# New joint order of the four engines within a step of the transformer layers: both projections directly behind the outputs, the feed-forward sum one position forward

## The reference, cut to what matters

```python
def attn_layer(x, Wqkv, qs, ksc, Wo):       # 6 layers of these two
    q, k, v = split(x @ Wqkv, 3)            # 16 heads of 64
    q, k = l2norm(q) * qs, l2norm(k) * ksc
    q, k = rotary(q, scale), rotary(k, 1 / scale)
    return local_attention(q, k, v) @ Wo    # windows of 32, looking one window back

def ffn_layer(x, g, bln, W1, b1, W2, b2):
    a, gate = split((layernorm(x) * g + bln) @ W1 + b1, 2)
    return a * gelu(gate) @ W2 + b2

def reference(x, ...):
    x = layernorm(x + first_attention(x))   # causal, only the diagonal of the softmax weighs v
    y = x
    for i in range(6):
        y = attn_layer(shift_tokens(y), ...) + y
        y = ffn_layer(shift_tokens(y), ...) + y
    return layernorm(x + y)
```

## Time and profile before

| | |
|---|---|
| median of 3 runs | 3484.91 us (3483.71 to 3487.97) |
| profiled execution | 3485.04 us, span of its instructions 3483.2 us |
| TensorE matmul busy | 3410.3 us, 98% |
| ScalarE busy | 3056.1 us, 88% |
| VectorE busy | 2991.3 us, 86% |
| GpSimd busy | 2494.3 us, 72% |
| DMA | 160.59 MB, mean 46 GB/s |
| granted TensorE clock, mean | 0.997 |

### The profile page before, as it was taken

How to read it: one execution, slowest core, us unless ns; L and a number is a source line. 1 busy time by engine, 2 the same in 40 slices (tenths; PEclk the granted TensorE clock), 3 DMA queues, 4 the chain that set the end, 5 groups by cost and what they waited for, 6 DMA issues and landing times. The chain is left out here.

```text
span 3483.2 us, 177745 instructions
## 1 busy us (share of the span) xinstructions
PE 3410.3 (98%) x70388; PEld 2881.8 (83%) x70388; DVE 2991.3 (86%) x7016; ACT 3056.1 (88%) x10549; POOL 2494.3 (72%) x2057
## 2 busy tenths in 40 slices
PE   8999999999999999999999999999999999999998
PEld 5666677888888888888888888888888888888877
DVE  8999988888888888888888888888888888888886
ACT  8999978898988888888888888888888889888886
POOL 0121178887878878788787887878888788887874
PEclk9999999999999999999999999999999999999999
DMA  2000011111211111121111121111211111111111
GB/s 105 8 5 20 5 53 53 48 42 43 57 55 50 44 44 46 54 57 48 46 44 50 52 57 47 43 42 54 59 48 46 43 47 54 45 46 47 51 42 44
DMA packets 177474, 160.59 MB, mean 46 GB/s; under 512 B 113933, under 2 KB 124813, under 8 KB 176397
## 3 DMA queue, kind: packets, MB, share of 16 engines
q1 hardware_dynamic: 176653, 149.22, 15.2%
HBM read 25.71 MB, written 4.19 MB: 9 GB/s over the span
## 5 line engine op out<-in xcount | busy, mean ns | idle before, releaser
L1544 POOL TENSOR_TENSOR a_rn<-a_ssqc,a_minus_half 128x16 f32<-128x16 f32 x384 | 1113.4, 2900 | 256.3 <-DVE a_ssqc L1751 252.1
L1428 ACT ACTIVATE late<-bank,a_negmax 128x64 f32<-128x64 f32 x3072 | 963.9, 343 | 31.0 <-DVE a_negmax L1705 29.4
L1562 POOL TENSOR_TENSOR a_r<-a_u,a_rn 128x512 f32<-128x512 f32 x768 | 800.7, 1043 | 55.9 <-DVE a_u L1733 10.5
L1428 ACT ACTIVATION_READ_ACCUMULATOR late<-bank,a_negmax 128x1 f32 x3072 | 728.6, 237 | 0.0
L1717 DVE TENSOR_TENSOR a_u<-bank,a_rot_c 128x512 f32<-128x512 f32 x768 | 524.7, 683 | 175.3 <-ACT a_sq L1404 174.7
L1551 POOL TENSOR_TENSOR a_PN<-late,a_erec 128x256 f32<-128x256 f32 x768 | 487.9, 636 | 255.8 <-DVE a_erec L1758 241.4
L1726 DVE TENSOR_TENSOR a_v<-bank,a_rot_s 128x512 f32<-128x512 f32 x768 | 522.7, 681 | 0.0
L1733 DVE TENSOR_TENSOR a_u<-a_u,a_v 128x1024 f32<-128x1024 f32 x384 | 469.7, 1223 | 25.6
L1404 ACT ACTIVATE a_sq<-bank 128x512 f32<-128x512 f32 x768 | 462.8, 647 | 17.2 <-PE bank L1013 16.7
L1411 ACT ACTIVATE a_QK<-bank 128x512 f32<-128x512 f32 x768 | 465.8, 607 | 4.1 <-PE bank L1054 1.9
L1054 PE MATMUL bank<-ident,a_r 128*128 128x128 f32 x3072 | 463.3, 274 | 5.2 <-ACT late L1396 1.8
(11 more groups left out here) (190 smaller groups left out, 7757.2 us busy)
## 6 DMA issues: line engine op xcount, KB each, us to landing
a_V_sh<-a_V_nat SPq DMA_DIRECT2D x384, 192.0 KB, 2.5
a_V_sh<-a_V_nat SPq DMA_DIRECT2D x192, 64.0 KB, 2.4
late<-in_qkv SPq DMA_DIRECT2D x20, 384.0 KB, 3.7
a_x_sh<-X SPq DMA_DIRECT2D x48, 128.0 KB
a_V_sh<-a_V_nat SPq DMA_DIRECT2D x192, 32.0 KB, 2.1
a_x_sh<-X SPq DMA_DIRECT2D x48, 127.0 KB
late<-X SPq DMA_DIRECT2D x47, 128.0 KB
late<-X SPq DMA_DIRECT2D x47, 127.0 KB
```

Of the source, the lines that this page charges most:

```text
L1428: ins = act.activation(E[:, s.par, k, :], scores[:, hp, col:col + KW], ACT.Exp, bias=negmax[:, s.par, k:k + 1], accum_out=esum[:, s.par, k ...
L1544: pool.tensor_tensor(rn[:, a.par, :], ssqc[:, a.par, :], minus_half[:, :], ALU.pow).then_inc(S["rn"], 1)
L1562: pool.tensor_tensor(heads(r[:, a.par, half]), heads(u[:, a.par, half]), rn[:, a.par, mm * 2 * HG:(mm + 1) * 2 * HG].unsqueeze(2).to_broad ...
```

## The change

The order within a step changes on all four engines. No instruction that computes is added or removed.

- TensorE: `project` of tile 1 follows `project` of tile 0 in every step (in steps 3 and 7 a piece of `up` stood between them). The other pieces come next, most of them ahead of `values`: in step 6 both `up`, in step 7 `transpose_x` and then `up`, in step 4 one ahead of `values` and the other too.
- ScalarE: `exps` (0,1) moves behind (1,1), so the copies of queries and keys (tile 0) and of the outputs come one group of exps earlier. `gelu` goes ahead of the squares, `gate_out` 1 behind both squares, `high_x` between them, the splits of weights ahead of `values` and `probs`.
- VectorE: `sines` before `cosines` for both tiles, with other work between them for tile 0; `clamp` behind both; `reciprocals` of head pair 1 earlier, of 0 at the end; `stats` behind `add`; `product` moved; `feed_forward_out` from the head of step 6 into the middle of step 5 (behind `add` and a reciprocal, ahead of `sines`, `cosines` and the other reciprocal).
- GpSimd: `units` of tile 1 first, `deviation` one step later.
- Waits: since the cosines now come last, `project` waits for them too (u_rot); the logits and the maxima wait for exp0 beside exp1; `sines` waits for the squares as `cosines` does.

The diff, without its hunk headers' context beyond the functions:

```diff
--- before.py
+++ after.py
@@ -1007,6 +1007,7 @@
                         pe.wait_ge(S["w_lo"], G * a.layer + a.g + 1)
                     ge(pe, S[f"sq{mm}"], a.k)
                     ge(pe, S[f"v_rot{mm}"], a.k)
+                    ge(pe, S["u_rot"], 2 * a.k - 1 + mm)
                     x, m = n % 2, slice((2 * a.half + mm) * P, (2 * a.half + mm + 1) * P)
                     pe.matmul(p_qk[mm][:, :], xh[:, x, m], wh[:, a.g, 0:2 * CQ], start=True, stop=False)
                     pe.matmul(p_qk[mm][:, :], xl[:, x, m], wh[:, a.g, 0:2 * CQ], start=False, stop=False)
@@ -1149,30 +1150,31 @@
                 late_end(n, p)
                 outputs(pair_at(n, p, LAG_O), n * NP + p, done(n, p - 1, LAG_T1))
                 project(n, p, 0)
+                project(n, p, 1)
+                if p == P_VALUES:
+                    up(n, p, 0, 1, p_ta)
+                if p == P_VALUES:
+                    up(n, p, 1, 1, p_tb)
+                if p == P_X and n + 1 < NI:
+                    transpose_x(n + 1)
+                if p == P_TURN:
+                    turn(n)
+                if p == P_GATES:
+                    up(n, p, 1, 0, p_ta)
+                if p == P_X:
+                    up(n, p, 2, 1, p_ta)
                 if p == P_GATE:
                     up(n, p, 0, 0, p_ta)
-                if p == P_X:
-                    up(n, p, 2, 1, p_ta)
-                project(n, p, 1)
-                if p == P_TURN:
-                    turn(n)
-                if p == P_VALUES:
-                    up(n, p, 0, 1, p_ta)
                 if p == P_GATES:
-                    up(n, p, 1, 0, p_ta)
+                    up(n, p, 2, 0, p_tb)
                 values(n, p)
                 late_pieces(n, p)
                 if p == P_BIAS:
                     shifts(n)
-                if p == P_X and n + 1 < NI:
-                    transpose_x(n + 1)
-                if p == P_VALUES:
-                    up(n, p, 1, 1, p_tb)
-                if p == P_GATES:
-                    up(n, p, 2, 0, p_tb)
                 if p == P_GELU:
                     down(n)
                 if s:
+                    ge(pe, S["exp0"], s.k)
                     ge(pe, S["exp1"], s.k)
                 logits(s, p_s)
                 transpose_probs(n, p)
@@ -1201,6 +1203,7 @@
                 if j == -3:
                     for name in ("sq0", "sq1", "v_rot0", "v_rot1"):
                         pe.wait_ge(S[name], NI * NP)
+                    pe.wait_ge(S["u_rot"], 2 * NI * NP)
                 else:
                     pe.wait_ge(S["exp1"], s.k if j == -4 else s.k - 1)
                 logits(s, end_s(s))
@@ -1443,32 +1446,32 @@
                     late_outputs(2 * p - 1)
                 queries_and_keys(pair_at(n, p, LAG_Q1), 1)
                 exps(s, 0, 0, p_s)
-                exps(s, 0, 1, p_s)
                 queries_and_keys(pair_at(n, p, LAG_Q0), 0)
                 exps(s, 1, 0, p_s)
                 outputs(pair_at(n, p, LAG_O))
                 exps(s, 1, 1, p_s)
+                if p < 2:
+                    split_up(n, p)
+                exps(s, 0, 1, p_s)
+                if p == P_GELU:
+                    gelu(n)
                 if p == P_TURN:
                     turned(n)
                 squares(n, p, 0)
+                if p == P_GATE:
+                    gate_out(n, 0, p_ta)
+                if p == P_X and n + 1 < NI:
+                    high_x(n + 1)
+                squares(n, p, 1)
                 if p == P_GATES:
                     gate_out(n, 1, p_ta)
-                if p == P_GELU:
-                    gelu(n)
-                if p == P_GATE:
-                    gate_out(n, 0, p_ta)
-                squares(n, p, 1)
                 if p == P_GATES:
                     gate_out(n, 2, p_tb)
-                if p == P_X and n + 1 < NI:
-                    high_x(n + 1)
-                values(n, p)
-                probs(pair_at(n, p, LAG_PT))
-                if p < 2:
-                    split_up(n, p)
                 split = split_at(n, p)
                 if split:
                     split_qkv(*split)
+                values(n, p)
+                probs(pair_at(n, p, LAG_PT))
 
             def end_exps(j, hp):
                 s = end_pair(j)
@@ -1564,13 +1567,13 @@
                                        ALU.mult).then_inc(S[f"r{mm}"], 1)
 
             def cycle(n, p):
+                units(pair_at(n, p, LAG_R + 1), 1)
                 probs(pair_at(n, p, LAG_S + 1), 0)
-                units(pair_at(n, p, LAG_R + 1), 1)
+                if p == P_NORM + 1 and n >= 2:
+                    deviation(n - 2)
                 probs(pair_at(n, p, LAG_S + 1), 1)
                 power(pair_at(n, p, LAG_R))
                 units(pair_at(n, p, LAG_R), 0)
-                if p == P_NORM and n >= 2:
-                    deviation(n - 2)
                 if p == 2 and n >= NI - 4:
                     last_deviation(n - NI + 4)
                 if (n, p) == (1, 0):
@@ -1701,6 +1704,7 @@
             def maxima(s, scores):
                 if s:
                     dve.wait_ge(S["logits"], s.k + 1)
+                    ge(dve, S["exp0"], s.k - 1)
                     ge(dve, S["exp1"], s.k - 1)
                     dve.tensor_reduce(negmax[:, s.par, :].rearrange("p (b i) -> p b i", b=2), scores.rearrange("p b (i k) -> p b i k", i=4), AX.X,
                                       ALU.max, negate=True).then_inc(S["max"], 1)
@@ -1720,7 +1724,10 @@
             def sines(a, mm):
                 if a:
                     m = 2 * a.half + mm
+                    dve.wait_ge(S[f"sq{mm}"], a.k + 1)
                     ge(dve, S["u"], a.k)
+                    if a.first and a.g == 0:
+                        ge(dve, S["rot"], MT * (a.layer - 1) + m + 1)
                     halves = lambda t: t.rearrange("p (s h t f) -> p s h t f", s=2, h=HG, t=2)
                     tab = rot_s[:, m, :, :].rearrange("p s (t f) -> p s t f", t=2).unsqueeze(2).to_broadcast([P, 2, HG, 2, DH // 2])
                     dve.tensor_tensor(halves(v[:, mm * 512:(mm + 1) * 512]), halves(p_qk[mm][:, :])[:, :, :, ::-1, :], tab,
@@ -1780,40 +1787,40 @@
 
             def cycle(n, p):
                 s, a, b = pair_at(n, p, LAG_S), pair_at(n, p, 0), pair_at(n, p, LAG_R)
-                if p == P_GELU + 1:
-                    feed_forward_out(n)
                 maxima(s, p_s)
                 norms(b)
+                sines(b, 1)
                 cosines(b, 1)
                 clamp(b)
-                sines(b, 1)
                 if p == P_X:
                     residual(n)
+                if p == P_TURN:
+                    norm(n)
+                add(b)
                 if p == P_NORM:
                     stats(n)
                 if p == P_TURN:
-                    norm(n)
-                add(b)
-                if p == P_X:
-                    product(n, 2, p_ta)
+                    turned(n)
+                reciprocals(s, 1)
                 if p == P_VALUES:
                     product(n, 0, p_ta)
-                if p == P_TURN:
-                    turned(n)
-                cosines(a, 0)
+                if p == P_VALUES:
+                    product(n, 1, p_tb)
+                if p == P_GELU:
+                    feed_forward_out(n)
                 sines(a, 0)
                 if p == P_BIAS:
                     biases(n)
+                if p == P_X:
+                    product(n, 2, p_ta)
                 if p == P_X and n + 1 < NI:
                     low_x(n + 1)
-                if p == P_VALUES:
-                    product(n, 1, p_tb)
+                if p == P_GATES:
+                    split_up(n)
+                cosines(a, 0)
                 reciprocals(s, 0)
-                reciprocals(s, 1)
                 if p in (P_TURN, P_GATES, P_GELU):
                     split_qkv(n, p)
-                if p == P_GATES:
-                    split_up(n)
                 if p == 3 and n >= NI - 4:
                     last_norm(n - NI + 4)
                 if p == 2 and n >= NI - 4:
```

## The result

| | before | after |
|---|---|---|
| median of 5 runs | 3484.59 us (3483.71 to 3487.97) | 3544.09 us (3542.22 to 3545.47) |
| profiled execution: span | 3483.2 us | 3542.3 us |
| TensorE busy | 3410.3 us | 3422.5 us |
| GpSimd busy | 2494.3 us | 2761.0 us |

The ratio is 1.0168 [1.0154, 1.0183]: 59.5 us slower, where the forecast was 24 us faster, and outside the range given. TensorE's mean granted clock is 0.996 for 0.997; by the granted clock of the two traces the lower level cost at most 14.1 us in after and 9.0 us in before, so it accounts for 5 us at most.

The account below looks back on a forecast made before the run. TensorE's instruction order was taken to set the pace, so only its gaps could be won. Terms -30 - 9 - 5 + 12 + 7.5 + 1 = -23.5, say -24 us, gave 3461 us; range 3444 to 3486.

Parts of the forecast that it names:

- the sentence on GpSimd: GpSimd: clamp 0.6 us later, transposes keep over half a microsecond of margin; priced nil, bounds 0 to 0.1 us a step.
- Deviation and normalisation: GpSimd's deviation moves one step on; normalisation in step 2 still finds it about 0.1 us ahead; priced nil.
- Step 2, priced at nothing: Step 2 of each iteration: no loss forecast, apart from +0.6 us once per layer for the qkv weights' low parts.
- step 6: TensorE's late starts around feed-forward and values matmuls vanish: 0.65 us in 46 iterations, -30 us, bounds 0 and -30.
- step 7: Next x transposed earlier, so TensorE's wait for VectorE's low part goes: 0.19 us in 46 iterations, -9 us.
- the edges: Second projection in steps 3 and 6 barely meets VectorE's cosines: +0.13 us each, 46 times, +12 us; bounds 0 to 0.4 each.
- the low weights: Low parts of qkv weights on VectorE, steps 2 and 5, five layers: 1.5 us each, +7.5 us, bounds 3 and 10.
- the high weights: Weights' high parts on ScalarE, moved ahead of values and probs, stop delaying a copy: -5 us, bounds 0 and -6.
- The first: Rival: VectorE 0.3 us later at steps 3 and 6, stalls 0.4 to 0.45 us, +40 instead of +12; chance 0.13.
- The second: Rival: added waits cost 0.11 to 0.18 us in each of 384 steps, 3503 to 3530 us; chance 0.15 with its like.
- a chain through ScalarE: Loss through ScalarE's order, priced at nil in the forecast; included in the second rival's chance of 0.15.
- The fourth: Rival: longer waits bring TensorE's clock another half-rate stretch, at most +7 us, 3468 us; chance 0.08.

Follow-up runs that it names:

- b_split: `b_clamp` with VectorE's `add` of 1024 columns cut into two of 512; 3497.94 us, ratio 1.0038.
- a_clamp: The kernel after, with only the clamp moved back between the two rotations of tile 1; 3473.26 us, ratio 0.9963.
- b_clamp: The kernel before, with only the clamp moved behind both rotations of tile 1; 3522.34 us, ratio 1.0104.
- a_pool: The kernel after, with only GpSimd's order as before (probs of head pair 0 first, deviation at the end of step 1); 3523.72 us, ratio 1.0116.
- b_gain: The kernel before, with only the moves for steps 6 and 7 and the waits for exp0; 3444.88 us, ratio 0.9885.
- b_waits: The kernel before, with only added TensorE waits: a third on each projection, a second ahead of the logits; 3482.31 us, ratio 0.9997.

## Why the prediction was wrong, point by point

- **The step that failed** is the sentence on GpSimd: "the clamp comes 0.6 us later ... the transposes wait for none of it by more than half a microsecond of margin ... Nil". The clamp's delay of 0.6 us was right, and of itself cost nothing in steps 0 and 3 (`b_split`). What was missed is beside what the instruction then runs: it starts with the `add` and is held for 0.96 us. This was outside the bounds given (0 to 0.1 us a step). `a_clamp` prices it at 71 us in the new order, `b_clamp` at 36 us in the old one.
- **Why it reaches TensorE.** GpSimd's work per step is 2 x 0.57 (probs) + 2 x 1.02 (units) + 3.03 (power) = 6.2 us. With 0.96 more (`power` in step 0) or 1.05 more (`probs` in step 1) it is 7.2, against 6.6 to 6.8 us of TensorE in these steps. It fits into steps 4 to 7, which last 7.7 to 9.3 us, and only just into step 3 (7.35), which still lost 0.43 us. A mean hid this: 72% over the whole span, and even the 81% of the middle of the layers (406 of 500 us) is a mean over short and long steps.
- **Deviation and normalisation.** "Finds the deviation about 0.1 us ahead" became a wait of 1.0 us in each iteration. `a_pool` gives back 20 us of the loss by the old order on GpSimd.
- **Step 2, priced at nothing.** Also with a short `power` (`a_clamp`), step 2 is 7.52 us for 7.12, 18 us in 46 iterations. Its timeline shows the same contention in the other direction. VectorE, then GpSimd, then TensorE of `a_clamp`:

```profile
1557.54 0.68 DVE L1733 TENSOR_TENSOR a_v<-bank,a_rot_s 128x512 f32<-128x512 f32 x1
1558.14 0.46 DVE L1758 TENSOR_SCALAR a_ssqc<-a_ssq 128x16 f32<-128x16 f32 x1
1558.51 0.68 DVE L1721 TENSOR_TENSOR a_u<-bank,a_rot_c 128x512 f32<-128x512 f32 x1
```

```profile
1556.98 1.00 POOL L1589 TENSOR_TENSOR a_rstd<-a_ve,a_minus_half 128x4 f32<-128x4 f32 x1
1557.96 0.61 POOL L1554 TENSOR_TENSOR a_PN<-late,a_erec 128x256 f32<-128x256 f32 x1
```

```profile
1558.32 0.50 PE L1012 MATMUL bank<-a_wh,a_xh 128*128 128x512 f32 x1
...
1559.34 0.47 PE L1012 MATMUL bank<-a_wh,a_xh 128*128 128x512 f32 x1
```

  The deviation, moved one step on, pushes `probs` beside the clamp. The clamp lasts 0.46 us for 0.16 and ends as `probs` does, the second rotation starts 0.37 us behind it instead of 0.07, and the second projection comes 1.02 us after the first, where 0.80 is usual. That the deviation alone does this was not run by itself, and it is not needed for such a meeting: in `b_split`, where it stands in its old place, the later clamp meets `probs` in the same step.
- **Right: step 6** (-0.65 us) **and step 7** (-0.19). In after, step 6 is 0.52 shorter, the forecast being 0.65 - 0.13 = 0.52; step 7 is 0.22 shorter. `b_gain`, with these moves only, gained 39.6 us where the two terms made 39.
- **Right in kind and nearly in size: the edges.** The feed-forward sum has its effect as walked: in `a_clamp` it starts at 1524.98 and the maxima at 1526.86, 1.88 us behind (1.89 forecast). In step 6 of after:

```profile
1558.67 0.50 PE L1012 MATMUL bank<-a_wh,a_xh 128*128 128x512 f32 x1
...
1559.48 0.48 PE L1012 MATMUL bank<-a_wh,a_xh 128*128 128x512 f32 x1
1559.80 0.39 PE L1013 MATMUL bank<-a_wh,a_xl 128*128 128x512 f32 x1
```

  The second projection is on the edge, 0.81 us behind the first, and its first matmul takes 0.32 for 0.23, the lost preload. In an ordinary iteration (the median between 1000 and 3000 us) steps 3 and 6 lose 0.07 and 0.09 us there in after and 0.15 and 0.17 in `a_clamp`, for 0.13 each: 3 us more than forecast. The means are higher (0.25 and 0.27 in `a_clamp`), but they hold the waits at the changes of layer, which are the next term.
- **Right: the low weights.** Between 1000 and 3100 us, with four changes of layer, TensorE waits 6.7 us in 8 times for the rotations in `a_clamp`, 1.7 us a change; 1.5 were forecast. **Right: the high weights.** The wait that cost 6.3 us is 0.3 us after.
- **Rivals.** None of the four explains the loss, and no rival had GpSimd. The first has a slip: its +4 on 3485 makes 3489, not 3487. The second had the right sign and a wrong mechanism (`b_waits`); its 0.15 did name "a chain through ScalarE". Its price was misread from the start: the matmul of 0.39 us at 1534.44, taken for one without the waits, is itself the first of a projection with two. The fourth occurred in `a_clamp`: in the last 382 us TensorE was granted a mean clock of 0.97, for 0.99 in before and 0.98 in after. What that cost was not isolated.

With the clamp where it was, the forecast is off by 12 us (3473 for 3461). Step 2 accounts for 18 and the edges for 3. Steps 1, 4 and 5 of `a_clamp` are 0.15 us shorter together, 7 us, of which the high weights were to bring 5; that leaves 19, and the 7 us between it and 12 are not explained.

## What to carry to other kernels

When an instruction of GpSimd is moved in time, ask what VectorE runs at the moment at which it will start, not only whether its result is in time: a start inside a long VectorE operation on two SBUF operands makes it last until that operation ends, and the other way round. Compare each engine's work with the length of the shortest steps, not with the mean, since that is where a seventh of a step more makes an engine with 81% load the bound. And a hand-written order is best changed in parts: here two parts (steps 6 and 7) were worth 40 us, and one line lost 71.

## What the runs showed of the hardware

- GpSimd's `power` on 128x16 values lasts 2.90 us alone, 3.81 to 3.93 when it starts 0.05 to 0.2 us (in a few cases 0.5) behind the start of an `add` of 1024 columns with two SBUF inputs (usually 1.22 us), 3.39 behind one of 0.7 us, and 2.90 again when it starts 0.62 us ahead of the `add`. At a lead of 0.22 us it lasted 2.90 or 4.20. This looks as if the operands were read only in its first few tenths of a microsecond; that is an inference, not shown.
- VectorE is held too: its clamp of 128x16 lasts 0.16 us alone and mostly 0.39 to 0.54 beside GpSimd's `probs`; its mean rose from 174 ns before to 204 in `a_clamp` and 267 in after:

```profile
L1758 DVE TENSOR_SCALAR a_ssqc<-a_ssq 128x16 f32<-128x16 f32 x384 | 102.6, 267 | 0.0
```

- A third wait on a matmul and a second one ahead of another, both met already, cost nothing in 384 steps (3482.3 for 3483.5 us, interval of 3 us to each side).
